# The last projection, layer norm, routing and expert stages of a four-layer transformer put into one program block

## The reference

```python
# L3_xattn, its end: attention output o (2048 x 256), then
x = x + (o @ Wo + bo)
# L3_ffn: top-1 routing over 8 experts, d_ff = 1024
xn = _layernorm(x)
router_probs = softmax(xn @ gate_w)              # gate_w: 256 x 8
expert_idx   = argmax(router_probs)
expert_w     = router_probs[expert_idx]
for e in range(8):
    h = gelu(xn @ w1[e] + b1[e]); y = h @ w2[e] + b2[e]
    out += where(expert_idx == e, expert_w, 0) * y
x = x + out
```

## Time and profile before

| | |
|---|---|
| median of 3 runs | 3333.82 us (3331.04 to 3334.6) |
| the profiled execution's own time | 3337.32 us |
| its span, first to last instruction | 3335.7 us |
| PE busy | 2891.0 us, 87% of the span |
| DVE busy | 2205.5 us, 66% |
| ACT busy | 1989.8 us, 60% |
| POOL busy | 1338.2 us, 40% |
| mean granted TensorE clock | 0.916 of full speed |

### The profile page before, as it was taken

How to read it: one execution, slowest core, us unless ns; L and a number is a source line. 1 busy time by engine, 2 the same in 40 slices (tenths; PEclk the granted TensorE clock), 3 DMA queues, 4 the chain that set the end, 5 groups by cost and what they waited for, 6 DMA issues and landing times. The chain is left out here.

```text
span 3335.7 us, 68908 instructions
## 1 busy us (share of the span) xinstructions
PE 2891.0 (87%) x26993; PEld 1989.8 (60%) x26994; DVE 2205.5 (66%) x3297; ACT 1989.8 (60%) x2962; POOL 1338.2 (40%) x979
## 2 busy tenths in 40 slices
PE   6769998765969998969998599788999999989678
PEld 3246666424436666536666498576666666667668
DVE  5968887678868884768884222767656565558455
ACT  3448887274548885548886111566666665547357
POOL 2249998120238886128886211660000000008233
PEclk8979998887979999979999699897999999999689
DMA  4511111200022220012221610102222222145556
GB/s 141 192 61 54 56 55 57 102 13 13 1 46 55 55 54 23 1 38 57 57 56 26 233 37 30 39 10 74 77 77 76 77 76 77 51 143 138 56 197 205
DMA packets 224950, 240.63 MB, mean 72 GB/s; under 512 B 137301, under 2 KB 175234, under 8 KB 217602
## 3 DMA queue, kind: packets, MB, share of 16 engines
q1 hardware_dynamic: 210167, 184.10, 19.7%
q0 software_dynamic: 12240, 49.83, 4.3%
q10 hardware_dynamic: 2233, 2.39, 0.2%
HBM read 146.16 MB, written 52.77 MB: 60 GB/s over the span
## 5 line engine op out<-in xcount | busy, mean ns | idle before, releaser
L2669 POOL TENSOR_TENSOR lta_p_lo<-lta_p,lta_p_hi 128x1024 f16<-128x1024 f32 x256 | 538.8, 2132 | 214.5 <-DVE lta_p_hi L2792 214.5
L2864 ACT ACTIVATE lta_p<-lta_banks,lw_gmax 128x512 f32<-128x512 f32 x512 | 324.5, 684 | 109.2 <-PE lta_banks L2707 105.7
L2775 DVE TENSOR_REDUCE lta_s_ps<-lta_s_ps 128x1 f32<-128x1101 f32 x240 | 314.2, 1309 | 101.1 <-PE lta_s_ps L2685 101.1
L4446 PE MATMUL m_h_ps<-m_x,m_w 128*128 128x512 f16 x1536 | 354.5, 381 | 3.2 <-issue 3.2
L4458 PE MATMUL m_y_ps<-m_w,m_hT 128*128 128x256 f16 x3072 | 355.8, 273 | 1.3 <-DVE m_hT L4618 1.3
L4458 PEld LDWEIGHTS m_y_ps<-m_w,m_hT 128*128 128x128 f16 x3072 | 299.2, 98 | 64.3 <-issue 7.1
L4543 ACT ACTIVATE m_h<-m_h_ps,m_h_bias,m_h_scale 128x512 f32<-128x512 f32 x256 | 199.3, 779 | 231.0 <-PE m_h_ps L4446 222.8
L1244 POOL TENSOR_TENSOR c0a_tri_p_lo<-c0a_tri_p,c0a_tri_p_hi 128x1024 f16<-128x1024 f32 (+2 forms) x192 | 285.7, 1522 | 60.1 <-DVE c0a_tri_p_hi L1418 59.0
L4618 DVE TENSOR_TENSOR m_hT<-m_h,m_hT 128x512 f16<-128x512 f32 x256 | 176.3, 692 | 200.7 <-ACT m_hT L4543 197.0
L4446 PEld LDWEIGHTS m_h_ps<-m_x,m_w 128*128 128x128 f16 x1536 | 150.9, 98 | 160.7 <-issue 7.4
L1493 ACT ACTIVATE c0a_tri_p<-c0a_banks,c_size 128x512 f32<-128x512 f32 (+3 forms) x384 | 209.1, 578 | 47.0 <-PE c0a_banks L1312 35.2
(11 more groups left out here) (818 smaller groups left out, 6590.1 us busy)
## 6 DMA issues: line engine op xcount, KB each, us to landing
m_w<-pw_w SPq DMA_DIRECT2D x23, 1024.0 KB
m_w<-in_L_ffn_w_dram SPq DMA_DIRECT2D x2, 8192.0 KB
m_raw<-in_L_ffn_W_dram SPq DMA_DIRECT2D x16, 1024.0 KB, 6.6
pwo_raw<-in_L_ffn_w_dram POOLq DMA_DIRECT2D x16, 1024.0 KB, 8.1
pw_w<-pwo_pair POOLq DMA_DIRECT2D x16, 1024.0 KB, 4.4
lta_q<-ltb_qT SPq DMA_DIRECT2D x96, 128.0 KB, 2.4
c_side<-in_fside_Bx16xSxS_dram SPq DMA_DIRECT2D x16, 616.0 KB, 4.8
c0a_tri_q<-c_near SPq DMA_DIRECT2D x96, 96.0 KB
```

The costliest lines, as they stand in the source:

```text
L2669: nc.gpsimd.tensor_tensor(p_lo[:, slot, :], p32[:, p32_slot(h, j), :], p_hi[:, slot, :], ALU.subtract).then_inc(rested, 1)
L2775: nc.vector.tensor_reduce(ntop_of(h)[:, n:n + 1], scores(h, n), AX_X, ALU.max, negate=True).then_inc(top_ready, 1)
L2864: nc.scalar.activation(p32[0:rows, slot, c * 512:(c + 1) * 512], t_ps[0:rows, c, :], ACT.Exp, bias=bias, scale=p["gmax"][0:rows, 0:1]).the ...
L4446: last = nc.tensor.matmul(h_ps[:, f % RING, :], w1[:, v, a, c, f * P:(f + 1) * P], x16[:, b, c, n * CHUNK:(n + 1) * CHUNK], start=c == 0 a ...
```

## The change

`c3o`, `m3r` and `m3e` become one block, `projected_routed_stage`, in which three functions add to every engine's program one behind the other: `project_rows` (new), `route_rows`, `paired_experts`. The attention output is written to a buffer `attended` that is allocated outside the attention stage, and `xn` is written over it tile by tile. One PSUM tile of all eight banks, `banks`, serves all three parts; in `project_rows` each of the PSUM roles has two banks. `lane_hot` lies over `hT`. The clears of the semaphores come after the whole block.

```diff
+def projected_routed_stage(nc, env, tag, name, args, rows, weight, bias, func, capacity, pairs, out):
...
+        r["banks"] = st.ps("banks", [P, 8, 512])
...
+        with nc.Block() as block:
+            project_rows(nc, env, Stage(nc, ctx, tag + "p"), block, w, weight, bias, r)
+            route_rows(nc, env, Stage(nc, ctx, tag + "r"), block, w, capacity, pairs, r)
+            paired_experts(nc, env, Stage(nc, ctx, tag + "e"), block, func, pairs, r, out)
+
+def project_rows(nc, env, st, block, w, weight, bias, r):
+    RING, CHUNK = 4, 4
+    GROUPS, BEHIND = TILES // CHUNK, 9
...
+    @block.sync
+    def _(sp):
...
+        sp.dma_start(bo[:], bias.partition_broadcast(P)).then_inc(bias_loaded, 16)
+        sp.dma_start(wo[:], weight.rearrange("(c p) n -> p c n", p=P)).then_inc(loaded, 16)
+        sp.dma_start(gate[:], w("gate_w").rearrange("(c p) e -> p c e", p=P)).then_inc(gate_loaded, 16)
...
+        store_x(0)
+        for g in range(1, GROUPS):
+            store_x(g)
+            store_rows(g - 1)
+        store_rows(GROUPS - 1)
...
+    @block.tensor
+    def _(pe):
...
+        def look(t):
+            if 0 <= t < TILES:
+                turn_normed(t)
+            if 0 <= t - 2:
+                gates(t - 2)
+        turn(0)
+        turn(1)
+        for t in range(TILES):
+            if t + 2 < TILES:
+                turn(t + 2)
+            project(t)
+            look(t - BEHIND)
+        for t in range(TILES - BEHIND, TILES + 2):
+            look(t)
+
+    @block.scalar
+    def _(act):
...
+        for t in range(TILES):
+            keep_rows(t)
+            if t >= 7 and t % CHUNK == 3:
+                root(t // CHUNK - 1)
+            if t >= BEHIND + 2:
+                keep_normed(t - BEHIND - 2)
+        for t in range(TILES - BEHIND - 2, TILES):
+            if t == TILES - BEHIND + 2:
+                root(GROUPS - 1)
+            keep_normed(t)
+
+    @block.vector
+    def _(dve):
...
+        for t in range(TILES):
+            add(t)
+            if t:
+                sum_row(t - 1)
+            if t >= 5 and t % CHUNK == 1:
+                spread_of(t // CHUNK - 1)
+            if t >= 7 and t % CHUNK == 3:
+                normalise(t // CHUNK - 1)
+        sum_row(TILES - 1)
+        spread_of(GROUPS - 1)
+        normalise(GROUPS - 1)

 def route_rows(...):
     @block.sync
     def _(sp):
-        sp.dma_start(gate[:], w("gate_w").rearrange("(c p) e -> p c e", p=P)).then_inc(gate_loaded, 16)
-        for g in range(TILES // 4):
-            sp.wait_ge(normed, 4 * (g + 1))
-            sp.dma_start(by_tile[:, 4 * g:4 * g + 4, 0:D], xn[:, 4 * g:4 * g + 4, :]).then_inc(rows_stored, 16)
         sp.wait_ge(weighted, 1)
         sp.dma_start(by_tile[:, :, 2 * D:2 * D + 1], weight[:].unsqueeze(2), allow_slow_non_contiguous=True).then_inc(w_stored, 16)
         sp.wait_ge(expert_ready, 1)
...
     @block.gpsimd
...
-        pool.wait_ge(pairs.x_stored, 16 * (TILES // 4))
-        pool.wait_ge(rows_stored, 16 * (TILES // 4))
+        pool.wait_ge(r["x_stored"], 16 * (TILES // 4))
+        pool.wait_ge(r["rows_stored"], 16 * (TILES // 4))
         pool.wait_ge(w_stored, 16)
         pool.wait_ge(ids_ready, 1)
```

More of the change, by code:

```diff
@@ L215, in _, with add_projection_stage @@
                         gate(t)
-def add_projection_stage(nc, env, tag, rows, weight, bias, beside=None, routed=None):
+def add_projection_stage(nc, env, tag, rows, weight, bias, beside=None):
     with ExitStack() as ctx:
@@ L3383, in paired_routed_stage @@
             r[n] = st.sb(n, [P, NT])
+        r["banks"] = st.ps("banks", [P, 8, 512])
         r["xs_loaded"] = [st.sem(f"xs_loaded{k}") for k in range(XS_RING)]
         r["w2_loaded"] = [st.sem(f"w2_loaded{k}") for k in range(W2_RING)]
[L3386 to L3389, removed]
+        for n in ("x_stored", "rows_stored", "lg_done"):
+            r[n] = st.sem(n)
@@ L3401, in load_reduction, with route_rows @@
     sp.dma_start(r["w2"][:, k, :], pairs.dram[1][bass.ds(e, 1)].rearrange("a p n -> p (a n)")).then_inc(r["w2_loaded"][k], 16)
-def route_rows(nc, env, st, ctx, w, capacity, pairs, r):
+def route_rows(nc, env, st, block, w, capacity, pairs, r):
     sb, ps, sem = st.sb, st.ps, st.sem
-    RING = 4
-    xn, xT, gate = sb("xn", [P, TILES, D]), sb("xT", [P, RING, DC, P]), sb("gate", [P, DC, E])
-    mean, var, rstd = (sb(n, [P, TILES]) for n in ("mean", "var", "rstd"))
     upto, all_ones = sb("upto", [P, P], BF16), sb("all_ones", [P, P], BF16)
@@ L3472, in _ @@
     def _(pe):
[L3473 to L3491, removed]
         pe.wait_ge(consts, CONSTS)
@@ L3514, in _ @@
     def _(act):
[L3515 to L3521, removed]
         act.wait_ge(shifted, 1)
@@ L3531, in _ @@
         reduce = lambda o, a, op: step(nc.vector.tensor_reduce(o, a, AX_X, op))
[L3533 to L3539, removed]
         dve.wait_ge(lg_done, TILES)
@@ L3607, in _, with paired_experts @@
             reduce(out[:], product[:], ALU.add)
-def paired_experts(nc, env, st, ctx, func, pairs, r, out):
+def paired_experts(nc, env, st, block, func, pairs, r, out):
     sb, ps, sem = st.sb, st.ps, st.sem
@@ L3787, in spread, with cross_attention_stage @@
     return ap.to_broadcast(shape)
[L3790 removed]
+def cross_attention_stage(nc, env, tag, args, name, mask, side, hides, combine=None, routed=None, into=None):
     w = lambda n: args[f"{name}_{n}"]
```

127 lines of the change are left out of this document (103 added, 24 removed).

## The result

| | before | after |
|---|---|---|
| median of 20 runs each | 3332.99 us (3328.12 to 3340.4) | 3326.77 us (3323.51 to 3331.83) |
| the profiled execution | 3337.32 us | 3325.06 us |
| its span | 3335.7 us | 3323.4 us |
| mean granted TensorE clock | 0.916 | 0.920 |

The ratio after to before is 0.9982, 95% interval 0.9975 to 0.9988: 6.2 us faster (4.0 to 8.3). Predicted were 3325.0 and a gain of 8.8, which lies just outside this interval.

The account below looks back on a forecast made before the run. The expert stage was taken as PE-bound, so only an earlier start could gain, with the stores holding the first gather after the change. Start -9.6 plus clears +0.8 gave -8.8: 3333.8 to 3325.0 us, range 3311 to 3330.

Parts of the forecast that it names:

- Gates earlier, worth nothing by themselves: Router gates beside the projection: logits at 3148, `ids` near 3164, 12 us saved of the visible chain, buying almost nothing.
- The stores hold the first gather, unchanged in time: Stores into `pw_rows`: rows still end at 3164.3, the weight at 3175.3, so the first gather is issued at 3176.5.
- Stores are no limit: Rival at POOL's wait: only `ids` or the last `xn` store holds the gathers; gain 22 us, 3312.1, chance 0.13.
- the first bracket: Sign at the first gather: what releases POOL's wait, forecast to be a DMA and not `ids`.
- Front clear +0.3: Before the projection: the attention's own semaphore clear now stands there, adding 0.3 us to everything.
- Start of the experts: First expansion at 3186.1 against 3195.74, 9.6 us earlier, since PE no longer waits for all seven gathers.
- Gathers held up: Rival at the expert start: gathers get through only behind `w2`'s 3 MB; gain under 6.7 us, chance 0.18.
- Tail +0.8: Behind the last scatter: clears of the first two parts move there, 0.4 us each, +0.8 together.
- Pace 5.52: Expert stage: 23 tiles after the first expansion run at 5.52 us each, as before.
- Pace lost: Rival in the expert stage: PE waits for `w2`, 0.7 us more per tile, 3341 us; chance 0.07.
- The sum: Whole kernel: -9.6 + 0.8 = -8.8 us, median 3333.8 to 3325.0.

Follow-up runs that it names:

- e3: Kernel after with the turns and gates beginning 14 tiles behind the projection instead of 9: 3317.28 us, 0.9969 of before.
- e5: Kernel before run once more, nothing edited, for a second trace: 3330.88 us (one run).
- the first trace: Profiled execution of the first comparison, here of the unedited kernel after: 3325.06 us; median of its 20 runs 3326.77 us, 0.9982 of before.
- e6: Kernel after with the router's weight stored from ACT's queue instead of SP's: 3317.92 us, 0.9957 of before.
- e4: Kernel after without the store of the router's weight, its column filled with ones during the attention: 3322.89 us, 0.9987 of before.
- e7: Kernel after with rows of 2112 bytes instead of 2052 and the weight written as 64-byte pieces: 3311.04 us, 0.9948 of before.
- e11: e7 with the first three tiles' w2 loads waiting for the landing of the second gather: 3304.66 us, 0.9936 of before.
- e8: Kernel after with the three parts' semaphores in one list, cleared once: 3318.47 us, 0.9963 of before.
- e1: Kernel after run again, nothing edited, beside the kernel before on the same chip: 3319.61 us, 0.9975 of before.
- e10: Kernel before with e7's edit, rows of 2112 bytes and the weight as 64-byte pieces: 3322.77 us, 0.9987 of before.

## Why the prediction was right, and where it was off

- *Gates earlier, worth nothing by themselves*: right, and shown by e3. The size was off. Logits came at 3141.3, on the old scale 3144.8, where 3148 was forecast; `ids` at 3160.6 for 3164. The gates of ten tiles ran at full clock (0.51 us for a tile's four matmuls, 0.86 at half), where the sum had all 16 at half. The waits were smaller than put down, 2.7 us in each of the first two groups and 2 for the root: PE stood idle 2.7 us in all between 3107 and 3141.3, 1.3 of it behind the last root.
- *The stores hold the first gather, unchanged in time*: right within 0.4 us (forecast 3176.5, measured 3173.35 + 3.5 = 3176.85), and the wait ended with the weight, as said. But the composition was not as said, and two errors cancelled: the last large store landed at 3171.4 on the old scale, 7.1 us later than the forecast 3164.3, and the small pieces ended 5 us behind it, not 11. In the other traces with old rows they ended 7 to 10 us behind, and in e5, where they were issued after the last store had landed, they took 11.5 us by themselves. In the first trace they passed beside the last large store, which took 12.7 us for it; e6 shows that the times add up whatever the queue. "Stores are no limit" fell with the first bracket. Its ground, that the DMA engines have room beside the small pieces, was right and did not help: the engines are done with them in 2 us, and it is the completion that comes 9 us later. e4 and e7 show what the rival would have needed.
- *Front clear +0.3*: `bo` is loaded 0.4 us later behind the attention's end. Right.
- *Start of the experts*: -9.6 forecast, -10.2 measured. The first gather was issued 0.35 us later than forecast, and from the second gather to the expansion it took 7.2 us instead of 8.1. "Gathers held up" didn't happen, but was half right as a cost: with the loads out of the way the turn comes 4.05 us behind the gather (e11), 2.9 us sooner than in the first trace of after (6.9) and 4.4 sooner than in e7. The forecast priced it only against the state before.
- *Tail +0.8*: mis-sized. From the last scatter's issue to the end it was 8.3 us and is 10.1, +1.8. Three clears less give 1.0 back (e8), 0.32 for each, near the low end of what was put down; that there are three more of them behind the last scatter and not two was miscounted. The other 0.8 is open.
- *Pace 5.52*: right; from the first expansion to the last scatter 131.3 us for 131.7. "Pace lost" fell.
- *The sum*: -10.2 - 0.4 + 1.8 = -8.8, the forecast number. That it is the same number is in part luck: the tail was mis-sized by 1.0 and the start by 0.6 the other way, with 0.4 from the pace. The medians say -6.2 [-8.3, -4.0] in the first comparison and -7.9 and -8.5 in the later ones. What the prediction didn't know: its trace was one of slower stores. It treated 5.97 us as a property of the kernel; e5 shows 19.9 us in place of 27.7 for the last store, and the early `ids` of the kernel before goes with it. Since both orders depend on the stores, the difference between them held while each moved by 6 us. That is luck again: with the quicker stores after's first gather is only 1.5 points earlier (70.2 in e5, 68.7 in e1), again nearly nothing, and not because `ids` was late but because the pieces were.

Open: why the completion of the small pieces comes 9 to 10 us behind their last packet; why the pace differs; 0.8 us of the tail. What holds the large pieces on the old pitch, the engines or what lies behind them, no run separates.

## What to carry to other kernels

When an earlier result buys nothing, read what else its consumer waits for before moving more work: one bracket, `ids` before and the weight's store after, decided what 16 us were worth. A DMA share near 1 at a quarter of the bandwidth seen elsewhere in the same trace is a fault of the pieces, not a full load, and they can be the pieces of a transfer ahead that is not yet complete. Look at the row pitch and the smallest column first. Rewriting a table's rows was worth here as much as the reordering (7.4 us on the new order, 4.9 on the old), and made the reordering worth half as much again. Put bulk loads behind the small transfer that starts the next stage.

## What the hardware showed beyond that

- Pieces of 1024 bytes on a pitch of 2052 bytes: 5.1 to 6.0 us per 512 KB in a row, 6.3 to 7.9 for the first; on 2112 bytes 2.9 us for the first. Pieces of 4 bytes, 2048 of them, took 11.5 us alone (e5) and ended 5 to 11 us behind the large stores; as 2048 pieces of 64 bytes on the new pitch they landed after 2.9 us (e10).
- The packets of the 4-byte pieces pass the DMA engines in 2 us (before), and the landing comes 9.8 us later. Until it does, loads queued behind them move at 75 to 79 GB/s (after, e1), without them at 395 (e7).
- The same store order ran at 5.97 and at 5.1 us per store, and a load of 8 KB queued behind them carried it to PE: 9.37 or 4.46 us of waiting for `gate`.
- A clear of semaphores at the end costs 0.32 us (three fewer, 1.0 us).
